# A metaformer layer on one core: the scaling moves to the front of VectorE's step, the square roots to the front of ScalarE's, and the convolution's bands are built inside the first steps

## The chip, the cores and the metric

The kernel runs on one core of a Trainium2 chip. The time is the device time of one execution in microseconds (us), read from the chip; lower is better. Three runs of the kernel before took 4016.77, 4024.47 and 4032.15 us. The engines are called by their short names: PE (TensorE, matmuls), ACT (ScalarE), DVE (VectorE), POOL (GpSimd) and SP (SyncE, which here only issues DMAs). Each runs its own instructions in the order in which they are written and waits for the others on semaphores.

## The reference

Input `x` is 32 images of 112 x 112 pixels with 96 channels, float32.

```
x = x + conv3x3_depthwise(_ln(x)) + _ln(x)     # _ln over the 96 channels, eps 1e-6
t = tokens(x)
h = relu(qlinear(_ln(t, 1e-5), W1, b1))        # 96 -> 384; inputs and weights rounded to 5 exponent, 2 mantissa bits
t = t + qlinear(h, W2, b2)                     # 384 -> 96, the same rounding; sums rounded to 16 bits
```

## The kernel before, in words

An image row index (112) lies on the partitions. A **chunk** is 8 image columns of one image, 112 x 8 x 96 values, 336 KB. An image has 14 chunks, and images go in pairs: 28 chunks (`UNIT`) to a pair, 448 chunks in all.

Each engine runs the same list of **steps** t, and one step works on several chunks at different stages. At step t:
- chunk t+30 is **normalised** for the convolution: DVE takes its mean and variance (`statistics` on `xn`, L582), ACT the square root (`deviation`, L485), DVE the reciprocal (`invert`, L612 to L618), and the eight columns are then written into `images`, columns 0 to 3 by ACT (`normalise`, L465, `ACT_COLS` = 4) and 4 to 7 by DVE (L640). `xn` has two buffers, so a load waits for the chunk before last to be normalised.
- some of the 96 channels of a pair are **convolved** on PE (`conv`, L384), 3 or 4 to a step. For each channel three float32 matmuls (six in the trace) multiply the pair's image by a banded 112 x 112 matrix. The bands of two channels (294 KB) are read from DRAM into a ring of three. ACT saves each finished pair of channels (`save_conv`, L475).
- chunk t-26 gets the convolution added to `x` on POOL (`add_conv`, L224).
- chunk t-28 goes through the **feed-forward**: DVE scales it to 8-bit floats (`scale`, L626), PE transposes it (`to_channels`, L339), ACT copies the result (`copy_xt`, L436), PE multiplies by W1 in three parts (`ffn1`, L352), ACT casts each (`cast_hid`, L444), DVE adds the bias (`add_bias`, L571) and rounds (`quantise`, L577), PE multiplies by W2 in two halves (`ffn2`, L365), ACT casts each (`cast_y`, L452), DVE adds the second bias (`add_y_bias`, L602) and POOL adds the result (`add_ffn`, L230).

Norm steps run from t = -30 to 417, convolutions from -2 to 445, feed-forward from 28 to 475. So there are five **stages**: norm alone (28 steps), norm and convolution (30), all three (t = 28 to 417, 390 steps), convolution and feed-forward (28), feed-forward alone (30).

Within a step the order is that of the code in each engine's `step`. On ACT it is: `copy_xt`, the rest of the last step's saves, `cast_hid` 0, `deviation`, a save, `cast_hid` 1, saves, `cast_y` 0 of the chunk before, `cast_hid` 2, `normalise`, `cast_y` 1. On PE it is: `to_channels`, one channel (of which the last third waits for `copy_xt`, `ffn1_free`), `ffn1` 0 and 1, two channels, `ffn1` 2, `ffn2` 0, any fourth channel, `ffn2` 1. POOL's `add_conv` waits until DVE has added the last bias of the step, and `add_ffn` for `add_y_bias`, so that POOL works beside DVE's `statistics` and `scale`.

Before the steps the banded matrices are built once: PE makes two of their columns for half of the channels at a time (`SETUPS`, L326), DVE and ACT copy them in turn (L563, L429) into the images' second buffer, and SP writes each half (7056 KB) to DRAM (L289). Nothing else may use that buffer meanwhile, and the second half's copies wait for the first half's write.

Of the kernel before, what the change touches and what calls it, by code (L numbers as in the profile page):

```python
# [24 lines left out]
FFN_RING = 7  # L25
ACT_COLS = 4
EPS_C = 1e-6
# [4 lines left out]
def metaformer(nc, x, conv_kernel, w1, b1, w2, b2, bands, out):  # L32
# [13 lines left out]
    with ExitStack() as ctx:  # L46
# [6 lines left out]
        def sem(name):  # L53
# [35 lines left out]
        STAGED_FROM = UNIT  # L89
        band_stage = images[:, 1, :, :, :].rearrange("p i c w -> p (i c w)")[:, 0:NB // 2 * H] \  # L90
            .rearrange("p (g n h) -> p g n h", g=GROUPS // 2, h=H)
        xf_flat = xf[:, :, :, :].rearrange("p r w c -> p (r w c)")
# [28 lines left out]
        band_ps = [bank[0:H, 0:SETUP_COLS * NB // 2] for bank in (conv_ps[:, 0], conv_ps[:, 1], y_ps)]  # L121

# [5 lines left out]
        band_col = [sem("band_col_dve"), sem("band_col_act")]  # L128
        bands_out = [sem(f"bands_out{i}") for i in range(2)]
        xn_in = [sem(f"xn_in{i}") for i in range(NORM_RING)]  # L130
# [54 lines left out]

        with nc.Block() as block:

            @block.gpsimd
            def _(pool):
# [22 lines left out]

                def add_conv(r, c, t):
# [6 lines left out]
                    if ffn_in(t - 1):  # L220
                        wait(pool, hid_biased, J * (LOOP * r + c - FFN_AT))
                    pool.wait_ge(xf_in[e % FFN_RING], dma_count(r, e, FFN_RING))
                    x2 = xf[0:H, e % FFN_RING]
                    pool.tensor_tensor(x2, x2, images[:, b, i, :, cols].rearrange("p c w -> p w c"), ALU.add).then_inc(with_conv, 1)  # L224

                def add_ffn(r, c):
                    e = c - FFN_AT
                    wait(pool, y_biased, LOOP * r + e + 1)
                    res = xf[0:H, e % FFN_RING]
                    pool.tensor_tensor(res, res, y[:, c % 2], ALU.add).then_inc(summed, CW)  # L230
# [10 lines left out]
            def _(sp):  # L241
# [38 lines left out]

                first = NORM_AT - 1
                for half in range(2):
                    for c in range(first, first + 2):
                        step(0, c, c)
                    first += 2
                    for s in band_col:
                        sp.wait_ge(s, SETUPS // 2 * (half + 1))
                    lo = GROUPS // 2 * half
                    sp.dma_start(bands[lo:lo + GROUPS // 2].rearrange("g h n k -> h g n k"), band_stage) \  # L289
                        .then_inc(bands_out[half], 16)  # L290
                for c in range(first, LOOP_AT):
# [14 lines left out]
            def _(pe):  # L306
# [12 lines left out]
                pe.wait_ge(prep, 31)  # L319
                for n in range(2 * SETUPS):  # L320
                    half, i = divmod(n, SETUPS)
                    if n >= 3:
                        pe.wait_ge(band_col[(n - 3) % 2], (n - 3) // 2 + 1)
                    for a in range(SETUP_COLS):
                        h = SETUP_COLS * i + a
                        mm = pe.matmul(band_ps[n % 3][:, NB // 2 * a:NB // 2 * (a + 1)],  # L326
                                       shift[:, H - 1 - h:2 * H - 1 - h],
                                       taps_16[:, NB // 2 * half:NB // 2 * (half + 1)], start=True, stop=True)
                    mm.then_inc(band_mm, 1)
                pe.wait_ge(w_copied, 2)  # L330
                for s in band_col:
                    pe.wait_ge(s, SETUPS)

# [34 lines left out]

                def conv(r, c, ch, next_waits):
                    m = (c - CONV_AT) // UNIT  # L370
                    g, i = divmod(ch, PAIR)
                    n = GROUPS * m + g
                    if i == 0:
                        if g == 0:
                            for s in normed:
                                wait(pe, s, LOOP * r + UNIT * (m + 1))
# [13 lines left out]
                def convs(r, c, t, lo, hi, next_waits=None):  # L390

                    chans = conv_channels(t)[lo:hi]
                    for ch in chans:
                        conv(r, c, ch, next_waits if ch == chans[-1] else None)
# [23 lines left out]
            def _(act):  # L418
# [4 lines left out]
                                     ACT.Identity).then_inc(w_copied, 1)  # L423
                for n in range(1, 2 * SETUPS, 2):
                    i = n % SETUPS
                    act.wait_ge(band_mm, n + 1)
                    if n == SETUPS + 1:
                        act.wait_ge(bands_out[0], 16)
                    nc.scalar.activation(band_stage[:, :, :, SETUP_COLS * i:SETUP_COLS * (i + 1)],  # L429
                                         band_ps[n % 3].rearrange("p (h g n) -> p g n h", h=SETUP_COLS, n=TAPS),  # L430
# [83 lines left out]
            def _(dve):  # L514
# [42 lines left out]
                dve.tensor_copy(b2q[:, :], b2_8).then_inc(prep, 1)  # L557
                for n in range(0, 2 * SETUPS, 2):
                    i = n % SETUPS
                    dve.wait_ge(band_mm, n + 1)  # L560
                    if n == SETUPS:
                        dve.wait_ge(bands_out[0], 16)
                    dve.tensor_copy(band_stage[:, :, :, SETUP_COLS * i:SETUP_COLS * (i + 1)],  # L563
                                    band_ps[n % 3].rearrange("p (h g n) -> p g n h", h=SETUP_COLS, n=TAPS)) \
                        .then_inc(band_col[0], 1)
# [56 lines left out]
                def scale(r, c):  # L622

                    e = c + 1 - FFN_AT
                    for w in range(CW):
                        op = dve.scalar_tensor_tensor(  # L626
                            out=xq_8[:, (c + 1) % 2, w // 2, 0:C, w % 2], in0=xf[0:H, e % FFN_RING, w, :],
                            scalar=stats[:, c % 2, 0, w, 1:2], in1=rstd_t[:, w:w + 1].broadcast_to([H, C]),
                            op0=ALU.subtract, op1=ALU.mult, saturate=False)
# [15 lines left out]
                def step(r, c, t):  # L645
                    now, before, after, norm = ffn_in(t), ffn_in(t - 1), ffn_in(t + 1), norm_in(t)
                    if before:
                        add_bias(r, c - 1, 2)
                    if after or norm:
                        statistics(r, c, t)  # L650
                    if before:
# [12 lines left out]

# [25 lines left out]
```

## Time and profile before

| | |
|---|---|
| median of 3 runs | 4024.47 us |
| the profiled execution | 4024.61 us |
| its span, first to last instruction | 4022.9 us |
| busy: DVE, PE, ACT, POOL | 90%, 78%, 73%, 43% |
| mean granted clock of TensorE | 0.966 of full |
| DMA | 714.60 MB, 178 GB/s over the span |

The busy share of an engine says how long it executed. It doesn't say who waited for whom. For that the profile has a chain of waits: from the last instruction back to what released it, and so on to the start. A timeline row gives the start, how long the group lasted, the engine, the line and, in brackets, how long the engine had been idle and what ended that.

### The profile page before, as it was taken

The numbers are of one execution on the slowest core, as the hardware profiler recorded it, in microseconds if no ns is written. First come the engines' busy times: TensorE is split into PE (matmuls) and PEld (weight loads), VectorE is DVE, ScalarE is ACT, GpSimd is POOL, SyncE is SP. The second block draws the span as 40 slices with busy tenths as digits, with TensorE's granted clock in tenths as the row PEclk, the third lists the DMA queues.
The fourth block names the chain that finished last, engine by engine and source line by source line (L and its number), as shares of the span: only waits on it lengthen the run. The fifth ranks groups of instructions, "written<-read, shape, count | busy, mean of one in ns | idle before, by whom it ended". The sixth has DMA issues, their size and how long they took to land.

```text
span 4022.9 us, 87017 instructions
## 1 busy us (share of the span) xinstructions
PE 3152.2 (78%) x24678; PEld 2482.8 (62%) x24678; DVE 3613.3 (90%) x12635; ACT 2935.4 (73%) x6204; POOL 1720.4 (43%) x915
## 2 busy tenths in 40 slices
PE   3088888878888788888888888888888888889977
PEld 2077666666666666666666666666666666667744
DVE  4647999999999999999999999998999999999998
ACT  3456777777777777777777777777777777777765
POOL 0002444444444444444444444444444444445555
PEclk9999999999999999999999999999999999999955
DMA  4466666666666666666666666666666666665533
GB/s 146 114 170 172 188 188 185 187 184 187 187 185 189 177 190 190 182 180 185 188 185 188 185 186 188 185 188 183 187 189 186 188 185 196 191 191 172 160 106 94
DMA packets 277321, 714.60 MB, mean 178 GB/s; under 512 B 34777, under 2 KB 34882, under 8 KB 276802
## 3 DMA queue, kind: packets, MB, share of 16 engines
q1 hardware_dynamic: 276802, 708.57, 60.1%
q8 instruction: 217, 3.56, 0.4%
q14 instruction: 302, 2.47, 0.2%
HBM read 539.84 MB, written 168.59 MB: 176 GB/s over the span
## 4 chain that ended last, share of the span: by engine, by line
PE 55%; ACT 31%; issue 7%; DMA 5%; DVE 1%; ACTq 1%; SPq 0%; POOLq 0%; POOL 0%; DVEq 0%
PE conv_ps L384 33%; ACT images L465 14%; PE hid_ps L352 13%; ACT hid L444 9%; PE y_ps L365 7%; ACT xt L436 4%; ACT y L452 4%; DMA band_ring<-bands 2%; DMA xn<-in_x 2%; ACTq L167 1%; DMA bands<-images 1%; PE conv_ps L326 1%; DVE stats L582 0%; PE y_ps L326 0%; PE xt_ps L339 0%
## 5 line engine op out<-in xcount | busy, mean ns | idle before, releaser
L384 PE MATMUL conv_ps<-images,band_ring 112*112 112x222 f32 (+1 forms) x9216 | 2064.9, 363 | 604.9 <-ACT xt L436 385.2
L384 PEld LDWEIGHTS conv_ps<-images,band_ring 112*112 112x112 f32 x9216 | 1568.0, 179 | 896.7 <-issue 656.7
L444 ACT ACTIVATE hid<-hid_ps 128x896 f16<-128x896 f32 x1344 | 1226.3, 913 | 505.2 <-PE hid_ps L352 505.2
L224 POOL TENSOR_TENSOR xf<-xf,images 112x768 f32<-112x768 f32 x448 | 980.3, 2188 | 1299.2 <-DVE hid L571 893.7
L230 POOL TENSOR_TENSOR xf<-xf,y 112x768 f32<-112x768 f32 x448 | 736.8, 1645 | 999.3 <-DVE y L602 997.7
L626 DVE SCALAR_TENSOR_TENSOR xq<-xf,stats,xt_ps 112x96 fp8e5<-112x96 f32 x3584 | 844.3, 310 | 0.0
L365 PE MATMUL y_ps<-w2t,hid 128*128 128x96 f16 x10752 | 634.5, 211 | 173.8 <-ACT y L452 172.3
L365 PEld LDWEIGHTS y_ps<-w2t,hid 128*128 128x128 f16 x10752 | 555.1, 100 | 329.0 <-ACT y L452 213.3
L465 ACT ACTIVATE images<-xn,neg_mean,rstd 112x96 f32<-112x96 f32 x1792 | 723.0, 545 | 13.2 <-DVE neg_mean L618 13.2
L352 PE MATMUL hid_ps<-xt,w1t 96*128 96x448 fp8e5 x2688 | 695.6, 369 | 27.7 <-ACT xt L436 19.5
L452 ACT ACTIVATE y<-y_ps 112x384 f16<-112x384 f32 x896 | 443.8, 495 | 364.4 <-PE y_ps L365 362.9
L582 DVE BATCH_NORM_STATS2 stats<-xn 112x6 f32<-112x192 f32 x1792 | 513.5, 348 | 79.5 <-DMA xn<-in_x 77.1
L571 DVE TENSOR_SCALAR hid<-hid,b1q 128x896 f16<-128x896 f16 x1344 | 528.1, 446 | 19.5 <-issue 9.1
L582 DVE BATCH_NORM_STATS2 stats<-xf 112x6 f32<-112x192 f32 x1792 | 510.6, 347 | 0.0
L577 DVE TENSOR_SCALAR hid<-hid 128x2688 uint16<-128x2688 int16 x448 | 505.3, 1128 | 0.1
L640 DVE TENSOR_SCALAR images<-xn,stats,rstd 112x96 f32<-112x96 f32 x1792 | 486.2, 367 | 0.0
L475 ACT ACTIVATE images<-conv_ps 112x448 f32<-112x448 f32 x768 | 414.4, 540 | 79.7 <-PE conv_ps L384 75.4
L352 PEld LDWEIGHTS hid_ps<-xt,w1t 96*128 96x128 f16 x2688 | 263.5, 100 | 237.1 <-ACT hid L444 31.8
L612 DVE RECIPROCAL xt_ps<-std 112x8 f32<-112x8 f32 x448 | 93.5, 209 | 197.2 <-ACT std L485 197.1
L485 ACT ACTIVATE std<-stats,eps 112x8 f32<-112x8 f32 x896 | 225.1, 295 | 57.5 <-DVE stats L582 57.3
L602 DVE TENSOR_TENSOR y<-y,b2q 112x768 f16<-112x768 f16 x448 | 250.7, 559 | 6.7 <-ACT y L452 3.0
L436 ACT ACTIVATE xt<-xt_ps 128x448 uint16<-128x448 uint16 x448 | 235.5, 526 | 11.2 <-PE xt_ps L339 11.2
(46 smaller groups left out, 571.1 us busy)
## 6 DMA issues: line engine op xcount, KB each, us to landing
band_ring<-bands SPq DMA_DIRECT2D x768, 294.0 KB, 5.2
xn<-in_x SPq DMA_DIRECT2D x448, 336.0 KB, 3.5
xf<-in_x SPq DMA_DIRECT2D x448, 336.0 KB, 4.8
out<-xf SPq DMA_DIRECT2D x448, 336.0 KB, 3.9
bands<-images SPq DMA_DIRECT2D x2, 7056.0 KB, 24.5
xf<-in_L_ffn_W SPq DMA_DIRECT2D x2, 144.0 KB, 2.8
xf<-in_L_conv_kernel SPq DMA_DIRECT2D x3, 3.4 KB
xf<-in_L_ffn_b SPq DMA_DIRECT2D x1, 42.0 KB, 3.4
```

The costliest lines, as they stand in the source:

```text
L224: pool.tensor_tensor(x2, x2, images[:, b, i, :, cols].rearrange("p c w -> p w c"), ALU.add).then_inc(with_conv, 1)
L230: pool.tensor_tensor(res, res, y[:, c % 2], ALU.add).then_inc(summed, CW)
L352: mm = pe.matmul(hid_ps[:, k, u, 0:HALF * H], w1t[:, P * j:P * j + P], xt_8[0:C, c % 2, HALF // 2 * u:HALF // 2 * (u + 1)], start=True, st ...
L365: mm = pe.matmul(y_ps[:, C * w:C * w + C], hid[:, c % 2, TOK * j + tok:TOK * j + tok + P], w2t[:, j, :], start=(j == 0), stop=(j == J - 1))
L384: mm = pe.matmul(dst[:, :, lo:hi], band_ring[:, n % BAND_RING, PAIR * dx + i, :], images[:, m % 2, :, ch, lo + dx - 1:hi + dx - 1], start= ...
L444: nc.scalar.activation(hid[:, c % 2, TOK * j:TOK * (j + 1)].rearrange("p (u n) -> p u n", u=2), hid_ps[:, k, :, 0:HALF * H], ACT.Identity) ...
L452: nc.scalar.activation(y[:, c % 2, HALF * u:HALF * u + HALF, :], y_ps[0:H, 0:HALF * C].rearrange("p (w c) -> p w c", c=C), ACT.Identity).t ...
L465: op = nc.scalar.activation(images[:, b, i, :, cols.start + w], xn[:, e % NORM_RING, w, :], ACT.Identity, bias=neg_mean[:, c % 2, w:w + 1] ...
L571: dve.tensor_scalar(part_j, part_j, b1q[:, j:j + 1], None, ALU.add).then_inc(hid_biased, 1)
L577: dve.tensor_scalar(bits.bitcast(U16), bits.bitcast(I16), ROUND8, -ROUND8, ALU.add, ALU.add).then_inc(hid_quant, 1)
L582: op = dve.bn_stats(stats[:, c % 2, i, w:w + 2, :].rearrange("p w s -> p (w s)"), src[:, w:w + 2, :].rearrange("p w c -> p c w"))
L626: op = dve.scalar_tensor_tensor(out=xq_8[:, (c + 1) % 2, w // 2, 0:C, w % 2], in0=xf[0:H, e % FFN_RING, w, :], scalar=stats[:, c % 2, 0, w ...
```

## The change

1. DVE's step. `scale` of a chunk ran at the end of the step before the one in which PE transposes it. It now runs in the same step, right behind `statistics`; it uses the statistics and reciprocals of the step before. The three `add_bias` of the chunk before come behind it together, then `quantise`, `invert`, `add_y_bias` and `normalise`.
2. ACT's step. `deviation` goes from behind `cast_hid` 0 to the front, ahead of `copy_xt`.
3. `ACT_COLS` goes from 4 to 5: ACT normalises five columns, DVE three.
4. POOL's step. `add_ffn` comes first and is one step later (chunk t-31); it waits until DVE has normalised the chunk before. `add_conv` follows and no longer waits for the bias.
5. The bands are built inside the first 23 norm steps, five setups to a step, four columns for a quarter of the channels each. The staging area holds two quarters, and SP writes four quarters (3528 KB each) to DRAM.

```diff
-ACT_COLS = 4
+ACT_COLS = 5
...
-        SETUP_COLS = 2
+        SETUP_COLS = 4
         SETUPS = H // SETUP_COLS
+        STEP_SETUPS = 5
...
+        def setups(c, t):
+            n = STEP_SETUPS * (t - NORM_AT)
+            return range(n, min(n + STEP_SETUPS, QUARTERS * SETUPS)) if c == t and n >= 0 else range(0)
...
-                def add_ffn(r, c):
-                    e = c - FFN_AT
+                def add_ffn(r, c, t):
+
+                    e = c - 3 - FFN_AT
+                    if norm_in(t - 1):
+                        wait(pool, normed[1], LOOP * r + c - NORM_AT)
                     wait(pool, y_biased, LOOP * r + e + 1)
...
                 def step(r, c, t):
+                    if ffn_in(t - 3):
+                        add_ffn(r, c, t)
                     if ffn_in(t + 2):
-                        add_conv(r, c, t)
-                    if ffn_in(t - 2):
-                        add_ffn(r, c - 2)
+                        add_conv(r, c)
...
+                    if c in done:
+                        q = done[c]
+                        for s in band_col:
+                            sp.wait_ge(s, SETUPS // 2 * (q + 1))
+                        sp.dma_start(bands[QGROUPS * q:QGROUPS * (q + 1)].rearrange("g h n k -> h g n k"),
+                                     band_stage[:, q % 2]).then_inc(bands_out[q], 16)
...
                     now, before, norm = ffn_in(t), ffn_in(t - 1), norm_in(t)
+                    for n in setups(c, t):
+                        if n % 2:
+                            build(n)
+                    if ffn_in(t + 1) or norm:
+                        deviation(r, c, t)
                     if now:
                         copy_xt(r, c)
                     save_conv(r, c - 1, t - 1, 3, C)
                     if now:
                         cast_hid(r, c, 0)
-                    if ffn_in(t + 1) or norm:
-                        deviation(r, c, t)
...
-                    if before:
-                        add_bias(r, c - 1, 2)
                     if after or norm:
                         statistics(r, c, t)
+                    for n in setups(c, t):
+                        if n % 2 == 0:
+                            build(n)
+                    if now:
+                        scale(r, c)
                     if before:
+                        for j in range(J):
+                            add_bias(r, c - 1, j)
                         quantise(r, c - 1)
                     if after or norm:
                         invert(r, c, t)
                     if ffn_in(t - 2):
                         add_y_bias(r, c - 2)
-                    if after:
-                        scale(r, c)
                     if norm:
                         normalise(r, c)
-                    if now:
-                        add_bias(r, c, 0)
-                        add_bias(r, c, 1)
```

On ACT, one step of the stage with all three, before (the rows L167 are register operations and waits of the sequencer; `std` is `deviation`, `xt` is `copy_xt`, `hid` is `cast_hid`, `images<-xn` is `normalise`):

```order
L452 ACTIVATE y<-y_ps 112x384 [waits y_mm]
L436 ACTIVATE xt<-xt_ps 128x448 [waits xt_mm]
L167 ISA
L167 ISA [waits hid_mm]
L444 ACTIVATE hid<-hid_ps 128x896 [waits y_mm]
L167 REGISTER_ALU
L485 ACTIVATE std<-stats,eps 112x8 [waits stats_done]
L485 ACTIVATE std<-stats,eps 112x8
```

The same place on ACT after the change:

```order
L461 ACTIVATE y<-y_ps 112x384 [waits y_mm]
L171 REGISTER_ALU
L494 ACTIVATE std<-stats,eps 112x8 [waits stats_done]
L494 ACTIVATE std<-stats,eps 112x8
L445 ACTIVATE xt<-xt_ps 128x448 [waits xt_mm]
L171 ISA
L171 ISA [waits hid_mm]
L453 ACTIVATE hid<-hid_ps 128x896 [waits y_mm]
```

The two square roots now stand between the last `cast_y` of one step and the `copy_xt` of the next.

On DVE, the same stage after the change, from the statistics to the normalising (before, `xq`, which is `scale`, stood between the `y` addition and `images<-xn`, and two of the three `hid<-hid,b1q` behind that):

```order
L594 BN_STATS stats<-xf 112x6 x3
L638 SCALAR_TENSOR_TENSOR xq<-xf,stats,xt_ps 112x96 x8
L171 ISA
L583 TENSOR_SCALAR hid<-hid,b1q 128x896 [waits hid_cast]
L171 REGISTER_ALU
L583 TENSOR_SCALAR hid<-hid,b1q 128x896 [waits hid_cast]
L171 REGISTER_ALU
L583 TENSOR_SCALAR hid<-hid,b1q 128x896 [waits hid_cast]
L589 TENSOR_SCALAR hid<-hid 128x2688 [waits hid_biased]
L171 REGISTER_ALU [waits xt_copied]
L624 RECIPROCAL xt_ps<-std 112x8 [waits std_done]
```

The reciprocals' wait for `xt_copied` now asks for the copy of a chunk that was scaled in the same step.

## Rows read from the trace of the kernel before

**Rows 1.** Page, part 1: busy time and share of the span of each engine.

```profile
PE 3152.2 (78%) x24678; PEld 2482.8 (62%) x24678; DVE 3613.3 (90%) x12635; ACT 2935.4 (73%) x6204; POOL 1720.4 (43%) x915
```

**Rows 2.** Page, part 4: the chain of waits, by engine and by line.

```profile
PE 55%; ACT 31%; issue 7%; DMA 5%; DVE 1%; ACTq 1%; SPq 0%; POOLq 0%; POOL 0%; DVEq 0%
PE conv_ps L384 33%; ACT images L465 14%; PE hid_ps L352 13%; ACT hid L444 9%; PE y_ps L365 7%; ACT xt L436 4%; ACT y L452 4%; DMA band_ring<-bands 2%; DMA xn<-in_x 2%; ACTq L167 1%; DMA bands<-images 1%; PE conv_ps L326 1%; DVE stats L582 0%; PE y_ps L326 0%; PE xt_ps L339 0%
```

**Rows 3.** Busy us by stretch: length, PE, PEld, DVE, ACT, POOL; clock, DMA, GB/s.

```profile
353.00:3603.00 3250.00, 2628.76 (x21158) 2091.34 (x21157) 3033.44 (x10854) 2498.66 (x5317) 1481.82 (x774) 0.99 0.64 186
```

**Rows 4.** The chain in order of time, one step: start, us, what.

```profile
2019.83 0.62 PE conv_ps L384 x2
2020.45 0.76 PE hid_ps L352 x4
2021.21 2.26 PE conv_ps L384 x12
2023.47 0.38 PE hid_ps L352 x2
2023.85 0.53 PE y_ps L365 x12
...
2027.60 0.43 ACT xt L436
...
2028.15 0.62 PE conv_ps L384 x2
```

**Rows 5.** Timeline of the same step, with rows of ACT, DVE and POOL.

```profile
2020.82 0.95 DVE L577 TENSOR_SCALAR hid<-hid 128x2688 uint16<-128x2688 int16 x1
...
2022.29 0.21 DVE L612 RECIPROCAL xt_ps<-std 112x8 f32<-112x8 f32 x1 [0.52 <-ACT std L485]
...
2024.98 1.08 DVE L640 TENSOR_SCALAR images<-xn,stats,rstd 112x96 f32<-112x96 f32 x4
...
2025.66 1.61 ACT L465 ACTIVATE images<-xn,neg_mean,rstd 112x96 f32<-112x96 f32 x4
...
2027.10 0.50 ACT L452 ACTIVATE y<-y_ps 112x384 f16<-112x384 f32 x1
2027.19 2.18 POOL L224 TENSOR_TENSOR xf<-xf,images 112x768 f32<-112x768 f32 x1 [2.14 <-DVE hid L571]
...
2030.09 0.49 ACT L485 ACTIVATE std<-stats,eps 112x8 f32<-112x8 f32 x2
2030.48 0.53 ACT L475 ACTIVATE images<-conv_ps 112x448 f32<-112x448 f32 x1
```

**Rows 6.** Timeline of the start: bands, first norm steps, first convolution.

```profile
13.31 0.72 PE L326 MATMUL conv_ps<-xf 67*112 67x144 bf16 x4 [5.34 <-DVE xf L546]
...
75.61 1.14 DVE L582 BATCH_NORM_STATS2 stats<-xn 112x6 f32<-112x192 f32 x4
...
109.07 1.15 DVE L582 BATCH_NORM_STATS2 stats<-xn 112x6 f32<-112x192 f32 x4 [19.93 <-DMA xn<-in_x]
...
178.42 1.15 DVE L582 BATCH_NORM_STATS2 stats<-xn 112x6 f32<-112x192 f32 x4 [1.07 <-DMA xn<-in_x]
...
185.31 1.15 DVE L582 BATCH_NORM_STATS2 stats<-xn 112x6 f32<-112x192 f32 x4 [1.01 <-DMA xn<-in_x]
...
193.93 9.01 PE L384 MATMUL conv_ps<-images,band_ring 112*112 112x224 f32 x36 [118.44 <-DMA band_ring<-bands]
```

**Rows 7.** Page, part 6: DMA issues, KB each, us from issue to landing.

```profile
xn<-in_x SPq DMA_DIRECT2D x448, 336.0 KB, 3.5
...
bands<-images SPq DMA_DIRECT2D x2, 7056.0 KB, 24.5
```

**Rows 8.** Timeline, feed-forward alone: `quantise` begun while POOL adds.

```profile
3902.72 2.00 DVE L577 TENSOR_SCALAR hid<-hid 128x2688 uint16<-128x2688 int16 x1
```

**Rows 9.** PE's timeline in the second stage, behind a wait for bands.

```profile
299.04 13.19 PE L384 MATMUL conv_ps<-images,band_ring 112*112 112x224 f32 x60 [2.50 <-DMA band_ring<-bands]
```

**Rows 10.** Busy time by stretch, just behind that wait.

```profile
300.00:304.00 4.00, 4.00 (x15) 3.38 (x14) 2.05 (x8) 1.50 (x4) 0.00 (x0) 0.57 0.59 167
```

More of the change, by code:

```diff
@@ L89, in metaformer @@
         STAGED_FROM = UNIT
-        band_stage = images[:, 1, :, :, :].rearrange("p i c w -> p (i c w)")[:, 0:NB // 2 * H] \
-            .rearrange("p (g n h) -> p g n h", g=GROUPS // 2, h=H)
+        QUARTERS = 4
+        QGROUPS = GROUPS // QUARTERS
+        QB = NB // QUARTERS
+        band_stage = images[:, 1, :, :, :].rearrange("p i c w -> p (i c w)")[:, 0:2 * QB * H] \
+            .rearrange("p (s g n h) -> p s g n h", s=2, g=QGROUPS, h=H)
         xf_flat = xf[:, :, :, :].rearrange("p r w c -> p (r w c)")
@@ L118, in metaformer @@
         b2_8 = staged(H, C).bitcast(F8)[:, 0:C]
-        SETUP_COLS = 2
+        SETUP_COLS = 4
         SETUPS = H // SETUP_COLS
-        band_ps = [bank[0:H, 0:SETUP_COLS * NB // 2] for bank in (conv_ps[:, 0], conv_ps[:, 1], y_ps)]
+        STEP_SETUPS = 5
+        band_ps = [bank[0:H, 0:SETUP_COLS * QB] for bank in (conv_ps[:, 0], conv_ps[:, 1], y_ps)]
         w1_in, w2_in, small_in, taps_sem = sem("w1_in"), sem("w2_in"), sem("small_in"), sem("taps_in")
@@ L128, in metaformer @@
         band_col = [sem("band_col_dve"), sem("band_col_act")]
-        bands_out = [sem(f"bands_out{i}") for i in range(2)]
+        bands_out = [sem(f"bands_out{i}") for i in range(QUARTERS)]
         xn_in = [sem(f"xn_in{i}") for i in range(NORM_RING)]
@@ L278, in step @@
                                 .then_inc(band_in[n % BAND_RING], 16)
[L281 to L291, printed above, removed]
+                done = {(SETUPS * (q + 1) - 1) // STEP_SETUPS + NORM_AT: q for q in range(QUARTERS)}
+                for c in range(NORM_AT - 1, LOOP_AT):
                     if c == CONV_AT - 1:
@@ L319, in _, with build @@
                 pe.wait_ge(prep, 31)
-                for n in range(2 * SETUPS):
-                    half, i = divmod(n, SETUPS)
+                pe.wait_ge(w_copied, 2)
+                def build(n):
+                    q, i = divmod(n, SETUPS)
                     if n >= 3:
@@ L325, in _ @@
                         h = SETUP_COLS * i + a
-                        mm = pe.matmul(band_ps[n % 3][:, NB // 2 * a:NB // 2 * (a + 1)],
-                                       shift[:, H - 1 - h:2 * H - 1 - h],
-                                       taps_16[:, NB // 2 * half:NB // 2 * (half + 1)], start=True, stop=True)
+                        mm = pe.matmul(band_ps[n % 3][:, QB * a:QB * (a + 1)], shift[:, H - 1 - h:2 * H - 1 - h],
+                                       taps_16[:, QB * q:QB * (q + 1)], start=True, stop=True)
                     mm.then_inc(band_mm, 1)
-                pe.wait_ge(w_copied, 2)
-                for s in band_col:
-                    pe.wait_ge(s, SETUPS)
                 def to_channels(r, c):
@@ L367, in ffn2, with conv @@
                     mm.then_inc(y_mm, 1)
-                def conv(r, c, ch, next_waits):
+                def conv(r, c, t, ch, next_waits):
                     m = (c - CONV_AT) // UNIT
@@ L374, in conv @@
                         if g == 0:
+                            if t == CONV_AT:
+                                for s in band_col:
+                                    pe.wait_ge(s, QUARTERS * SETUPS // 2)
                             for s in normed:
@@ L393, in convs @@
                     for ch in chans:
-                        conv(r, c, ch, next_waits if ch == chans[-1] else None)
+                        conv(r, c, t, ch, next_waits if ch == chans[-1] else None)
                     if next_waits and not len(chans):
@@ L423, in _, with build @@
                                      ACT.Identity).then_inc(w_copied, 1)
-                for n in range(1, 2 * SETUPS, 2):
-                    i = n % SETUPS
+                def build(n):
+                    q, i = divmod(n, SETUPS)
                     act.wait_ge(band_mm, n + 1)
-                    if n == SETUPS + 1:
-                        act.wait_ge(bands_out[0], 16)
-                    nc.scalar.activation(band_stage[:, :, :, SETUP_COLS * i:SETUP_COLS * (i + 1)],
+                    if q >= 2 and i == 1:
+                        act.wait_ge(bands_out[q - 2], 16)
+                    nc.scalar.activation(band_stage[:, q % 2, :, :, SETUP_COLS * i:SETUP_COLS * (i + 1)],
                                          band_ps[n % 3].rearrange("p (h g n) -> p g n h", h=SETUP_COLS, n=TAPS),
@@ L557, in _, with build @@
                 dve.tensor_copy(b2q[:, :], b2_8).then_inc(prep, 1)
-                for n in range(0, 2 * SETUPS, 2):
-                    i = n % SETUPS
+                def build(n):
+                    q, i = divmod(n, SETUPS)
                     dve.wait_ge(band_mm, n + 1)
-                    if n == SETUPS:
-                        dve.wait_ge(bands_out[0], 16)
-                    dve.tensor_copy(band_stage[:, :, :, SETUP_COLS * i:SETUP_COLS * (i + 1)],
+                    if q >= 2 and i == 0:
+                        dve.wait_ge(bands_out[q - 2], 16)
+                    dve.tensor_copy(band_stage[:, q % 2, :, :, SETUP_COLS * i:SETUP_COLS * (i + 1)],
                                     band_ps[n % 3].rearrange("p (h g n) -> p g n h", h=SETUP_COLS, n=TAPS)) \
@@ L622, in scale @@
                 def scale(r, c):
-                    e = c + 1 - FFN_AT
+                    e = c - FFN_AT
                     for w in range(CW):
                         op = dve.scalar_tensor_tensor(
-                            out=xq_8[:, (c + 1) % 2, w // 2, 0:C, w % 2], in0=xf[0:H, e % FFN_RING, w, :],
-                            scalar=stats[:, c % 2, 0, w, 1:2], in1=rstd_t[:, w:w + 1].broadcast_to([H, C]),
+                            out=xq_8[:, c % 2, w // 2, 0:C, w % 2], in0=xf[0:H, e % FFN_RING, w, :],
+                            scalar=stats[:, (c - 1) % 2, 0, w, 1:2], in1=rstd_t[:, w:w + 1].broadcast_to([H, C]),
                             op0=ALU.subtract, op1=ALU.mult, saturate=False)
@@ L646, in step @@
                     now, before, after, norm = ffn_in(t), ffn_in(t - 1), ffn_in(t + 1), norm_in(t)
-                    if before:
-                        add_bias(r, c - 1, 2)
                     if after or norm:
                         statistics(r, c, t)
+                    for n in setups(c, t):
+                        if n % 2 == 0:
+                            build(n)
+                    if now:
+                        scale(r, c)
                     if before:
+                        for j in range(J):
+                            add_bias(r, c - 1, j)
                         quantise(r, c - 1)
```

9 lines of the change are left out of this document (4 added, 5 removed).

## Prediction

> **What bounds the kernel now.** I read the busy shares first, then the chain of waits, then one step of the chain against the timeline. The busy shares say DVE: 90% of the span [rows 1], and in the stage where all three kinds of work run, 3033 of 3250 us [rows 3]. The chain of waits says something else: PE 55%, ACT 31%, DVE 1% [rows 2]. DVE is busy, and almost nothing that ends last goes through it.
>
> The Trainium skill (Perfetto Trace Analysis, Identifying the Most-Contended Engine) has you take the engine with the highest occupancy and optimise that one first. That would be DVE. This trace doesn't bear it out, and that is the main choice of this prediction.
>
> One step of the chain shows why. `copy_xt` ends on ACT and PE, held at the last third of its first channel, goes on at 2019.83: 0.62 us of convolution, 0.76 of `ffn1` 0 and 1, 2.26 of two channels, 0.38 of `ffn1` 2, 0.53 of `ffn2` 0 [rows 4], together 4.55 us with no gap. Then ACT takes over and works through, in its own order, `cast_y` 0, `cast_hid` 2, the four columns of `normalise`, `cast_y` 1 and the next `copy_xt`, whose link begins at 2027.60, and PE goes on at 2028.15. That is a closed loop of 2028.15 - 2019.83 = 8.32 us, and there is nothing in it that waits for DVE. 390 steps of 8.32 are 3245 us, which is the length of the stage [rows 3]: the loop is the stage. DVE itself waits in each step, 0.52 us for the square roots [rows 5]; its own work is 8.32 - 0.52 = 7.80 us.
>
> Two things of ACT's are outside the loop today. The saves stand in places where ACT waits for PE, and so does `deviation`: it sits behind `cast_hid` 0, where ACT has time until `ffn2` 0 is done. Moving it costs or brings something only by where it lands.
>
> **The change part by part.** *`deviation` to the front of ACT's step.* It now stands between `cast_y` 1 and `copy_xt`, both links of the loop. From the start of the two square roots to the start of what follows them it is 2030.48 - 2030.09 = 0.39 us [rows 5]. Its input is there: DVE's statistics end some 2 us into its step and ACT comes to it later. ACT has no wait in that part of the loop that could swallow it, so +0.39 us a step. The bounds: 0 if ACT waited at that place for PE's transposes, 0.49 (the row's whole duration) if nothing overlaps. I take 0.39.
>
> *A fifth column on ACT.* Four columns take 2027.10 - 2025.66 = 1.44 us from start to start [rows 5], 0.36 each, all of it in the loop: +0.36 us. Bounds 0.36 and 1.61 / 4 = 0.40. DVE loses one of four columns, 1.08 / 4 = 0.27 us [rows 5], off the loop: nothing.
>
> *`scale` behind the statistics, biases together.* On DVE this only reorders; its work becomes 7.80 - 0.27 = 7.53 us, and its wait for the square roots goes. What it must deliver in time is `scale` before `to_channels` and `quantise` before `ffn2` 0. `scale` ends about 4 us into DVE's step and the transposes follow at once, while ACT reaches `copy_xt` only after the square roots; `quantise` ends about 2 us after `scale`, and PE comes to `ffn2` 0 4.0 us of its own work behind `copy_xt`. Neither is late. `invert` now waits for the `copy_xt` of the same step; what is queued behind it on DVE is the second bias, three columns and the next statistics, and ACT needs the reciprocals only for `normalise`, some 6 us later. So: nothing gained, since the loop doesn't use DVE, and nothing lost while DVE's 7.53 us plus new stalls stay under the loop's length.
>
> *POOL.* Its two additions, 1.64 and 2.18 us, now run one behind the other from the end of DVE's normalising. They are beside statistics and `scale`, together about 4 us. Where they run over, DVE's bias or rounding is held: `quantise` takes 2.00 us [rows 8] when it begins beside POOL's addition and 0.95 otherwise [rows 5]. A late `xf` would do it. One such stall a step, 1.05 us, makes DVE 8.6 us, still under the new loop. Nothing; it is at the edge of mattering.
>
> *The `xn` load.* A chunk's load is issued once ACT has normalised the chunk two before it, and lands 3.5 us later [rows 7]. From there DVE needs statistics, `scale` and the transposes, about 4.5 us, before `copy_xt`: 8 us, against one loop and the `cast_y` and square roots before it, about 9.8 us. Hidden, by less than 2 us. SP's queue: the output's DMA now waits for an addition made in the same step, and the `xf` and band loads stand behind it; but SP waits longer at the `xn` load ahead of all three, so that wait hides the other.
>
> So a step of the main stage becomes 8.32 + 0.39 + 0.36 = 9.07 us. Times 390: 0.75 x 390 = +292 us.
>
> *The other stages.* In the two without normalising only one square root is moved, half of 0.39, in 58 steps: at most 11 us where ACT's turn is in the chain; I take +8 (bounds 0 and 11). In the second stage the chain passes ACT's columns only now and then: between 0 and 30 x 0.36 = 11 us, I take +5.
>
> *The bands.* Before: from 13.31 to 75.61 they are built, 62.3 us, of which 24.5 is the wait for the first half's write [rows 7]; from 75.61 to 193.93 the 28 norm steps, 118.3 us, with 19.93 of waiting behind the second write [rows 6]. Two norm steps take 185.31 - 178.42 = 6.89 us [rows 6]. After: if the building hides wholly in the norm steps' waits, 28 x (3.45 + 0.18) = 102 us, plus four writes of a quarter, each 12.2 us by size, of which 24.5 - 19.93 = 4.6 are covered as today: 4 x 7.7 = 31. With the first load that is some 135 us in place of 180.6, a gain of 46. If it adds to them wholly, 62.3 - 24.5 = 37.8 us come back, a gain of 8. The setups now hold four small matmuls in place of two, which no row prices; DVE's and ACT's copies alternate and so wait for each other. I take the middle, -25 (bounds -46 and -8, and 0 if the small matmuls bound it).
>
> **The sum**, against the profiled execution, 4024.61 us (0.1 us above the median; the span is 1.7 less): 4024.6 + 292 + 8 + 5 - 25 = 4305 us, 7% slower.
>
> **The rivals.** *DVE bounds it.* This is what the skill's rule on occupancy would give; worked out from rows: with the wait gone and a column less the step is 7.53 us, 0.79 less, 390 x 0.79 = 308 us, and with the bands 4024.6 - 308 - 25 = 3692 us. For it: 90% busy, and 0.52 us of waiting in each step. Against it: the chain, and that DVE's wait is for ACT, which the change makes later and not earlier in the loop. 6%.
>
> *Half of the cost is hidden.* If PE's transposes come late, ACT would have waited at `copy_xt` and the square roots fill that time: only the column counts, 0.36 x 390 = 140, and 4024.6 + 140 + 13 - 25 = 4153 us. Against it: before, ACT doesn't wait there. 6%.
>
> *The two halves cancel.* If the square roots are hidden and the column's end is where PE waits anyway, the sum is the bands' alone, near 4005 us. 2%.
>
> *PE's clock falls.* The main stage has a granted clock of 0.99 [rows 3]. In the second stage, behind a wait of 2.50 us, a stretch had 0.57 [rows 9, 10], a mix of the full and the half level. PE's wait for `copy_xt` grows by up to 0.75 us in each step. If the clock came to 0.9 on average, PE's 4.55 us would be 0.5 longer: 390 x 0.5 = +197, near 4500 us. Against it: today's gaps in the main stage, over a microsecond each, left it at 0.99. It decides from the point where the gap gets as long as the one in that row. 5%.
>
> **How the numbers follow.** The forecast has 81%: 4305 us. Its own range is 4240 to 4385: a step cost of 0.65 to 0.90 (254 to 351 us; the ends are small overlaps, and a stall of DVE that shows) and the bands. With a part of the clock's case and of the hidden half the range is 4200 to 4400, which leaves out under 2 in 10. A difference of 0.5%, 20 us, is about what a measurement of this kernel can tell from none. Slower by more: 81 + 6 + 5 = 92%. Faster by more: 6%. Between: 2%.
>
> **What would show it.** Right: in the main stage `copy_xt` follows its neighbour every 9.0 to 9.1 us; the chain still has PE and ACT, now with the square roots' line at 4% and the columns' line near 17%; DVE's busy share falls to about 83% although its work is hardly changed, with waits for `xt_copied` or `xn`; the first convolution starts near 170 us. Wrong: a step below 8.3 us with DVE without waits (then DVE was the bound); the square roots missing from the chain; ACT waiting for the transposes (PE's line L339 before `copy_xt`); a granted clock well under 0.99 in that stage; the first convolution after 194 us.

## The result

| | us |
|---|---|
| before, median of 4 runs | 4020.62 |
| changed, median of 4 runs (4662.08 to 4752.31) | 4694.22 |
| ratio | 1.165, 95% interval 1.159 to 1.171 |
| forecast (range) | 4305 (4200 to 4400) |
| profiled execution of the changed kernel, and its span | 4708.99, 4707.3 |

The change makes the kernel 16.5% slower. The sign was forecast, the size was not: 674 us were lost, 280 were foreseen, and the time lies outside the range. One of the four runs of the changed kernel, 4752.31 us, lies more than 1.5% above the fastest and is left out of the ratio; the median of the other three is 4679.44, and the differences to other runs below are taken from it.

The page of the changed kernel, busy shares and the chain of waits, beside [rows 1, 2]:

```profile
PE 3576.7 (76%) x24902; PEld 2754.8 (59%) x24902; DVE 3721.2 (79%) x12187; ACT 3100.4 (66%) x6652; POOL 1725.4 (37%) x915
...
PEclk9998888888888989899888999889898888989965
...
PE 52%; ACT 32%; issue 8%; DMA 3%; DVE 3%; ACTq 1%; POOL 1%; SPq 0%; POOLq 0%; DVEq 0%
PE conv_ps L391 33%; PE hid_ps L356 13%; ACT images L474 13%; ACT hid L453 7%; PE y_ps L369 6%; ACT xt L445 4%; ACT y L461 4%; ACT std L494 3%; DMA xn<-in_x 2%; DMA band_ring<-bands 1%; DVE stats L594 1%; ACTq L171 1%; POOL xf L229 1%; DVE xq L638 1%; DVE images L652 0%
```

The square roots (L494) are in the chain now, as forecast. The surprise is the clock row: it is 8 or 9 tenths through the main stage, which before had 0.99 [rows 3]. The stretch that answers to it (length, busy us of PE, PEld, DVE, ACT, POOL, then clock, DMA share, GB/s):

```profile
353.00:4280.00 3927.00, 3029.13 (x21070) 2334.12 (x21069) 3153.48 (x10423) 2639.80 (x5681) 1486.64 (x773) 0.89 0.52 153
```

One step of the chain in order of time (start, us, what), beside [rows 4]:

```profile
2023.00 0.62 PE conv_ps L391 x2
2023.63 0.76 PE hid_ps L356 x4
2024.38 2.26 PE conv_ps L391 x12
2026.64 0.38 PE hid_ps L356 x2
2027.02 0.53 PE y_ps L369 x12
...
2030.81 0.32 ACT y L461
2031.13 0.39 ACT std L494 x2
2031.51 0.43 ACT xt L445
2031.95 0.12 issue
2032.07 0.62 PE conv_ps L391 x2
```

PE's links are those of before to the hundredth. ACT's have the two square roots between `cast_y` 1 and `copy_xt`, and 2032.07 - 2023.00 = 9.07 us, which is the forecast step. But not every step is like this. Of 388 intervals between successive `copy_xt` in the main stage, 174 are 8.9 to 9.1 us, 160 are 10.4 to 10.8 and 46 are 12.2 to 12.4; the mean is 10.17 (before: 8.37, of which 375 of 388 are 8.2 to 8.4). This is how a longer one begins, in PE's rows of the timeline; after the shape stands the idle time before, and what ended it. The first three rows are of a step two earlier and come into play below:

```profile
2020.40 0.37 PE L343 MATMUL xt_ps<-ident,xq 112*128 112x112 bf16 x4 [0.59 <-DVE xq L638]
...
2023.00 0.62 PE L391 MATMUL conv_ps<-images,band_ring 112*112 112x222 f32 x2 [1.43 <-ACT xt L445]
...
2024.22 2.42 PE L391 MATMUL conv_ps<-images,band_ring 112*112 112x224 f32 x12
...
2038.55 0.37 PE L343 MATMUL xt_ps<-ident,xq 112*128 112x112 bf16 x4 [0.60 <-DVE xq L638]
2038.76 0.97 PE L391 MATMUL conv_ps<-images,band_ring 112*112 112x224 f32 x4
2041.14 1.08 PE L391 MATMUL conv_ps<-images,band_ring 112*112 112x222 f32 x2 [1.41 <-ACT xt L445]
2042.01 1.70 PE L356 MATMUL hid_ps<-xt,w1t 96*128 96x448 fp8e5 x4
2043.50 4.45 PE L391 MATMUL conv_ps<-images,band_ring 112*112 112x224 f32 x12
2047.79 0.54 PE L356 MATMUL hid_ps<-xt,w1t 96*128 96x448 fp8e5 x2
```

and the granted clock (the third number from the end) in stretches of both:

```profile
2022.00:2024.00 2.00, 1.00 (x5) 0.66 (x6) 1.74 (x6) 0.87 (x4) 0.00 (x0) 1.00 0.50 81
2024.00:2026.00 2.00, 2.00 (x13) 1.85 (x11) 1.34 (x6) 1.88 (x3) 1.05 (x1) 1.00 1.00 393
...
2038.00:2040.00 2.00, 1.18 (x8) 0.80 (x8) 1.97 (x7) 2.00 (x7) 0.82 (x1) 1.00 0.00 0
2040.00:2042.00 2.00, 0.86 (x2) 0.60 (x3) 1.52 (x5) 1.01 (x4) 0.00 (x0) 0.70 0.44 58
2042.00:2044.00 2.00, 2.00 (x7) 1.20 (x6) 1.36 (x6) 0.92 (x2) 0.92 (x1) 0.50 1.01 379
```

The twelve convolution matmuls take 4.45 us in place of 2.42 because the clock fell to its lower level (0.50 is 1.2 of 2.4 GHz). They are links of the loop, so the whole delay goes into the step. Before it fell PE had been idle twice, 0.60 us for `scale` and 1.41 for `copy_xt`; but two steps earlier it had been idle for 0.59 and 1.43 us at the same places, and the clock stayed at 1.00. Three steps earlier one longer wait had done nothing either; the clock's stretches from 2012 to 2020 show 1.00:

```profile
2013.93 0.62 PE L391 MATMUL conv_ps<-images,band_ring 112*112 112x222 f32 x2 [1.84 <-ACT xt L445]
```

The trace settles whether the longer steps are those with a fallen clock. All of the 214 have the lower level in them, for 1.6 us or more; of the 174 others eight have, for 0.5 us each. The 214 are together 429 us longer than 9.07 us each. The kernel before had 13 steps over 9.5 us, 12 of them with a fall: 27 us together with the stage's first.

In sum, by the starts of `copy_xt`: the first comes at 331.2 us in place of 351.0 (-20), the 390th at 4285.1 in place of 3611.6 (3954 against 3261 us, +693), and from there to the end of the span it is 422 against 411 us (+11). Together +684, the difference of the two spans. Of the 693 us, 0.75 x 390 = 292 are the forecast step and some 400 (429 - 27) the steps with a fallen clock.

### The profile page after: what moved, and what is told of

It is laid out like the page before. It is cut to its first block, busy times and chain, and to the rows that moved or that the text cites. A ratio compares the mean times of both kernels' runs of the same rounds, so it can differ in the third digit from the quotient of the medians.

```text
span 4707.3 us, 87416 instructions
## 1 busy us (share of the span) xinstructions
PE 3576.7 (76%) x24902; PEld 2754.8 (59%) x24902; DVE 3721.2 (79%) x12187; ACT 3100.4 (66%) x6652; POOL 1725.4 (37%) x915
## 4 chain that ended last, share of the span: by engine, by line
PE 52%; ACT 32%; issue 8%; DMA 3%; DVE 3%; ACTq 1%; POOL 1%; SPq 0%; POOLq 0%; DVEq 0%
PE conv_ps L391 33%; PE hid_ps L356 13%; ACT images L474 13%; ACT hid L453 7%; PE y_ps L369 6%; ACT xt L445 4%; ACT y L461 4%; ACT std L494 3%; DMA xn<-in_x 2%; DMA band_ring<-bands 1%; DVE stats L594 1%; ACTq L171 1%; POOL xf L229 1%; DVE xq L638 1%; DVE images L652 0%
## 5 line engine op out<-in xcount | busy, mean ns | idle before, releaser
L391 PE MATMUL conv_ps<-images,band_ring 112*112 112x222 f32 (+1 forms) x9216 | 2362.7, 401 | 701.8 <-ACT xt L445 621.0
L391 PEld LDWEIGHTS conv_ps<-images,band_ring 112*112 112x112 f32 x9216 | 1790.8, 204 | 1071.8 <-issue 770.6
L453 ACT ACTIVATE hid<-hid_ps 128x896 f16<-128x896 f32 x1344 | 1200.8, 914 | 605.4 <-PE hid_ps L356 605.4
L474 ACT ACTIVATE images<-xn,neg_mean,rstd 112x96 f32<-112x96 f32 x2240 | 883.6, 544 | 14.2 <-DVE neg_mean L630 14.2
L583 DVE TENSOR_SCALAR hid<-hid,b1q 128x896 f16<-128x896 f16 x1344 | 782.4, 624 | 113.3 <-ACT hid L453 110.1
L356 PE MATMUL hid_ps<-xt,w1t 96*128 96x448 fp8e5 x2688 | 818.3, 422 | 33.1 <-ACT xt L445 24.8
L356 PEld LDWEIGHTS hid_ps<-xt,w1t 96*128 96x128 f16 x2688 | 293.8, 111 | 302.8 <-issue 109.7
L652 DVE TENSOR_SCALAR images<-xn,stats,rstd 112x96 f32<-112x96 f32 x1344 | 381.1, 368 | 29.5 <-POOL xf L229 29.4
L589 DVE TENSOR_SCALAR hid<-hid 128x2688 uint16<-128x2688 int16 x448 | 390.9, 873 | 15.3
L343 PE MATMUL xt_ps<-ident,xq 112*128 112x112 bf16 x1792 | 172.3, 221 | 131.3 <-DVE xq L638 127.0
L494 ACT ACTIVATE std<-stats,eps 112x8 f32<-112x8 f32 x896 | 223.4, 293 | 29.1 <-DVE stats L594 22.9
```

Source lines behind the costliest of these rows:

```text
L356: mm = pe.matmul(hid_ps[:, k, u, 0:HALF * H], w1t[:, P * j:P * j + P], xt_8[0:C, c % 2, HALF // 2 * u:HALF // 2 * (u + 1)], start=True, st ...
L391: mm = pe.matmul(dst[:, :, lo:hi], band_ring[:, n % BAND_RING, PAIR * dx + i, :], images[:, m % 2, :, ch, lo + dx - 1:hi + dx - 1], start= ...
L453: nc.scalar.activation(hid[:, c % 2, TOK * j:TOK * (j + 1)].rearrange("p (u n) -> p u n", u=2), hid_ps[:, k, :, 0:HALF * H], ACT.Identity) ...
L474: op = nc.scalar.activation(images[:, b, i, :, cols.start + w], xn[:, e % NORM_RING, w, :], ACT.Identity, bias=neg_mean[:, c % 2, w:w + 1] ...
L583: dve.tensor_scalar(part_j, part_j, b1q[:, j:j + 1], None, ALU.add).then_inc(hid_biased, 1)
```

## The experiments

Theory 1 is the prediction's loop of ACT and PE with the clock added to it: what the change puts into the loop costs 0.75 us a step, and PE's longer idle times let the clock fall, which costs the rest. The rivals are that DVE bounds the kernel, and that the slow steps come from a late load or from DVE's and POOL's new order. Ratios are to the kernel before on the same chip, with 95% intervals.

**A column less on ACT.**

```diff
-ACT_COLS = 5
+ACT_COLS = 4
```

> The changed kernel with ACT_COLS back at 4. Theory 1 (a closed loop of ACT and PE sets the step, 0.39 us of square roots and 0.36 us of a fifth column are in it, and PE's longer idle time lets its clock fall in some steps): the undisturbed step is 9.07 - 0.36 = 8.71 us, PE waits 0.3 to 0.4 us less for copy_xt, the granted clock lies between 0.89 and 0.97, time 4200 to 4450 us. Theory 2 (DVE, POOL or a late load sets the slow steps): DVE has a column more, 0.27 us, and the time stays within 1% of 4690 us or grows.

Measured: 4251.16 us, ratio 1.056 (1.051 to 1.061), clock 0.945 over the span. 307 of the steps are 8.6 to 8.7 us, the mean is 9.02. As theory 1 has it: one column is worth 428 us, of which 140 by the step's length and the rest by the clock (65 steps are over 9.5 us here, 64 of them with a fall, and 214 in the changed kernel).

**More work for PE while it waits.**

```diff
                     for dx in (1, 0, 2):
                         if dx == 2 and next_waits:
+                            if busy:
+                                keep_busy(n % 2)
                             next_waits()
...
+                def keep_busy(k):
+                    for _ in range(24):
+                        pe.matmul(conv_ps[:, k, PAIR * IMGS * W:], ident[:, :], ident[:, 0:512 - PAIR * IMGS * W],
+                                  start=True, stop=True, skip_group_check=True)
```

(`busy` is true for the first channel of a step in the main stage. The extra matmuls write spare columns of the bank in which the channel is being summed. With them the kernel's output is wrong, by a relative error of 0.34; why was not followed up, and this run and the two like it are read for time alone.)

> The changed kernel, with 24 extra matmuls (128 x 128 by 64 columns, results unused) on PE in every step of the main stage, placed just before PE waits for copy_xt. They add work and no dependence. Theory 1: PE's idle time there falls from 1.4-1.8 us to a few tenths, the granted clock is 0.97 or more, nearly every step is 9.07 us, time 4280 to 4330 us. Theory 2 (the slow steps come from a late load or from DVE and POOL, and the clock falls because PE then waits): the steps of 10.4 to 12.3 us stay, time within 1% of 4690 us or more.

Measured: 4325.95 us, 1.074 (1.070 to 1.079), clock 0.964. 351 of 388 steps are 8.9 to 9.1 us. PE's rows of one step in its timeline:

```profile
2014.43 0.37 PE L343 MATMUL xt_ps<-ident,xq 112*128 112x112 bf16 x4 [0.41 <-DVE xq L645]
2014.64 0.97 PE L398 MATMUL conv_ps<-images,band_ring 112*112 112x224 f32 x4
2015.45 0.86 PE L355 MATMUL conv_ps<-ident 128*128 128x64 bf16 x24
2016.86 0.62 PE L398 MATMUL conv_ps<-images,band_ring 112*112 112x222 f32 x2 [0.55 <-ACT xt L452]
2017.32 0.92 PE L361 MATMUL hid_ps<-xt,w1t 96*128 96x448 fp8e5 x4
2018.08 2.42 PE L398 MATMUL conv_ps<-images,band_ring 112*112 112x224 f32 x12
```

PE does 0.86 us more work in every step and the kernel is 353 us faster. Nothing in the loads, DVE's order or POOL's was touched. This is the run that tells the clock from the other causes: with PE kept busy nearly all the slow steps are gone.

**The control: the same extra matmuls in the kernel before.** The edit is the one above.

> The kernel before with the same 24 extra matmuls in each step of the main stage: the control for the run that added them to the changed kernel. Theory 1 (they act through the clock alone): before has few steps with a fallen clock, so at most those go; the step stays 8.32 us, time between 0 and 25 us below before. If the extra matmuls brought time in some other way, or cost it, this run would show it: over 0.6% faster, or slower.

Measured: 4049.02 us, 1.007 (1.005 to 1.009), clock 0.966. It was slower, which I had not expected: the extra matmuls cost 30 us here, some steps being 8.5 to 9.2 us. They bring nothing by themselves. Without that cost, if it is the same there, the changed kernel with its clock kept up would be near 4326 - 30 = 4296 us; the forecast without the clock's case was 4305.

**Five columns in the kernel before, no order changed.**

```diff
-ACT_COLS = 4
+ACT_COLS = 5
```

> The kernel before with ACT_COLS = 5 and nothing else: no engine's order is changed, and DVE has less work. Theory 1: the undisturbed step is 8.32 + 0.36 = 8.68 us, at least 390 x 0.36 = 140 us slower; PE's wait for copy_xt grows by as much and some steps lose more by the clock, time 4160 to 4400 us. Theory 2 (DVE bounds the kernel before, and the slow steps come from the new order): 0.27 us less on DVE, time 3920 to 4030 us, clock as before.

Measured: 4300.3 us, 1.069 (1.065 to 1.073), clock 0.938. 240 steps are 8.7 us, 73 are 10.4, and every step over 9.5 us has a fall of the clock in it. DVE had less to do and the kernel was 280 us slower: DVE doesn't bound it, and the clock falls without any of the new orders.

**The same with the extra matmuls.**

> The kernel before with ACT_COLS = 5 and the 24 extra matmuls in each step of the main stage. Theory 1: without the extra matmuls this kernel was at 4300 us, of which 390 x 0.36 = 140 us is the column and some 140 us the clock. With them the undisturbed step is 8.68 to 8.75 us, steps of 10 us and more become few, time 4165 to 4210 us. Rival (the 10 us steps have another cause): 4300 us or, with the cost of the extra matmuls, 4330 us.

Measured: 4184.74 us, 1.041 (1.039 to 1.043), clock 0.967; 304 steps of 8.7 us. 116 us come back. Less the 30 of the control it is 4155, against 4018 + 140 for the column alone. So in this kernel too the column's cost is half its own length and half the clock.

**`deviation` back at its old place in the changed kernel.**

```diff
                 def step(r, c, t):
...
-                    if ffn_in(t + 1) or norm:
-                        deviation(r, c, t)
                     if now:
                         copy_xt(r, c)
                     save_conv(r, c - 1, t - 1, 3, C)
                     if now:
                         cast_hid(r, c, 0)
+                    if ffn_in(t + 1) or norm:
+                        deviation(r, c, t)
```

> The changed kernel with deviation back behind cast_hid 0, all else as changed. If the 0.39 us of the square roots were all that its new place costs, the step is 9.07 - 0.39 = 8.68 us and the time near that of the kernel before with five columns, 4300 us. But with DVE's new order a second loop closes: scale 1.88, transposes 0.41, copy 0.64, PE to the end of ffn1 0 1.2, cast_hid 0.81, square roots 0.54, reciprocals to normalise 1.6, statistics 2.1, and scale again, 9.2 us. Theory 1 expects that loop to end last: an undisturbed step of 9.1 to 9.3 us, DVE waiting for the square roots and no longer for xt_copied, the clock as low as in the changed kernel or lower, time 4650 to 4850 us.

Measured: 4681.24 us, 1.166 (1.162 to 1.169), clock 0.869. 105 steps are 9.2 us and 87 are 9.3 to 9.4. The waits (who waited for what: us in total between 500 and 3500, times, longest):

```profile
DVE xt_ps L624 <- ACT std L494: 696.7, 298, 3.2
PEld xt_ps L343 <- DVE xq L638: 523.6, 293, 2.7
PE xt_ps L343 <- DVE xq L638: 514.5, 298, 7.7
```

The second loop is there, with the length worked out from rows: `scale`, transposes, copy, `ffn1`, cast, square roots, reciprocals, statistics, `scale`. So the 0.39 us can't simply be undone. With DVE's new order the square roots are either ahead of `copy_xt`, in ACT's loop, or behind it, in DVE's. The prediction hadn't seen this.

**The bands alone.** The bands are built inside the steps as in the change; `ACT_COLS` and every engine's order are those of before.

> The bands built inside the first 23 norm steps, in quarters, with all engines' step orders and ACT_COLS = 4 as before: the one part of the change that brought time. Theory 1: the first convolution starts near 170 us in place of 194, later stages are unchanged, time 15 to 30 us below the kernel before (3990 to 4005 us). Rival: the gain of 20 us at the start is given back in the second stage, where PE waits for bands, and the time is within 5 us of before.

Measured: 3994.0 us, 0.993 (0.991 to 0.996). The first convolution starts at 164.5 us (changed kernel: 168.4, before 193.9 [rows 6]). This part of the change is a gain of 0.7% by itself.

**One column less than before on ACT, one more on DVE**, on the kernel with the bands in the steps (`ACT_COLS = 3`).

> The kernel before with the bands built in the steps, and three columns on ACT, five on DVE. Theory 1: the loop loses 0.36 us (7.96 us), DVE gains 0.27 (7.80 to 8.07 us) and so ends last; step 8.05 to 8.15 us, DVE's wait for the square roots nearly 0, time 3890 to 3920 us. Rival (DVE bounds the kernel before): 390 x 0.27 = 105 us slower than the 3994 us of the same kernel with four columns.

Measured: 3862.17 us, 0.962 (0.960 to 0.965); 312 steps of 8.0 us. It is 28 us below the forecast's low end. The chain, by engine:

```profile
DVE 69%; PE 15%; issue 7%; ACT 4%; DMA 3%; SPq 0%; DVEq 0%; ACTq 0%; POOLq 0%
```

More work on the engine that was 90% busy made the kernel 3.3% faster, until most of the chain went through that engine. The median step is 7.97 us, where DVE had been expected at 8.07 and the loop of ACT and PE at 7.96. Two things explain the tenth: a column costs DVE 0.24 us from start to start and not the 0.27 of the row, and DVE's own work is nearer 7.74 than 7.80, as the next run shows. The two loops are level here.

**Two of ACT's four columns where ACT waits**, on the kernel with the bands in the steps (`normalise` now takes the bounds of its columns).

```diff
+                    if norm:
+                        normalise(r, c, 0, 2)
                     if before:
                         cast_y(r, c - 1, 0)
                     if now:
                         cast_hid(r, c, 2)
                     if norm:
-                        normalise(r, c)
+                        normalise(r, c, 2, ACT_COLS)
```

> The kernel before with the bands built in the steps, and two of ACT's four normalising columns moved ahead of cast_y 0, into the time in which ACT waits for ffn2 0 (nothing is added or taken away). Theory 1 (ACT's columns are in the loop only because of where they stand): two columns, 0.72 us, leave the loop, which would be 7.6 us; DVE's own work of 7.80 us then ends last, so the step is 7.8 to 7.9 us, DVE's wait for the square roots goes to nearly 0, PE waits less and the clock stays, time 3790 to 3830 us. Rival (any work of ACT is on the path, wherever it stands): the step stays 8.32 us, time 3994 us.

Measured: **3784.07 us, 0.942 (0.939 to 0.945)**, the fastest kernel of the study. ACT's and DVE's rows at that place in its timeline:

```profile
2011.70 0.20 DVE L627 RECIPROCAL xt_ps<-std 112x8 f32<-112x8 f32 x1
...
2012.49 0.90 ACT L474 ACTIVATE images<-xn,neg_mean,rstd 112x96 f32<-112x96 f32 x2
...
2013.54 0.49 ACT L460 ACTIVATE y<-y_ps 112x384 f16<-112x384 f32 x1 [0.15 <-PE y_ps L368]
2013.93 0.91 ACT L452 ACTIVATE hid<-hid_ps 128x896 f16<-128x896 f32 x1
```

The two columns stand where ACT had waited for `ffn2` 0 (in the kernel before 267.4 us in 357 waits between 500 and 3500, 0.75 us each); 0.15 of that wait is left. DVE hardly waits for the square roots any more, 16 us in all between 500 and 3300 us. The mean step is 7.84 us, the median 7.74, and DVE, with 57% of the chain, now ends last in most places; 7.80 for its own work was a little too much. Nothing was taken away: the same instructions on the same engines, two of them a place earlier.

**Three of five columns there.** As above with `ACT_COLS = 5` and `normalise(r, c, 0, 3)` first.

> As the run with two columns moved ahead of cast_y 0, but ACT_COLS = 5 and three of the five moved. Theory 1: the ACT and PE loop is 8.32 + 0.36 - 3 x 0.36 = 7.6 us, DVE's own work 7.80 - 0.24 = 7.56 us; the two are now equal, so a step of 7.6 to 7.85 us and 3700 to 3790 us, at most a few per cent below the 3784 us of the run with two columns. Rival (ACT's own work, 6.4 + 0.4 us and its waits, ends last once more than two columns stand there): slower than that run, 3790 to 3900 us.

Measured: 3837.21 us, 0.955 (0.953 to 0.957). It is slower than the run before it, as the rival had it, and the chain goes through ACT (44%) and hardly through DVE (6%). 157 of 388 steps are 7.6 us, as the two loops allow, and 136 are 8.2. In the one step of the chain that I followed, a save stands ahead of the three columns and ACT has no wait left to hide the third in; that this is the cause in all 136 was not tried.

## Why the prediction was wrong

*What bounds the kernel: right.* DVE, 90% busy, was off the path. It is shown from both sides: less work for DVE and more for ACT cost 7%, more for DVE and less for ACT brought 3.3%. The rival by the Trainium skill's rule on occupancy (Perfetto Trace Analysis, Identifying the Most-Contended Engine), 3692 us, failed with it.

*The step of 9.07 us: right.* It is the length of the undisturbed step to the hundredth, by 0.39 for the square roots and 0.36 for the column, 8.72 with the column left out of the change, and 8.68 with the column alone in the kernel before. The square roots alone were not run: their 0.39 is read from the chain and is what remains above 8.32 in the changed kernel with four columns (0.40). One sign was off all the same: the columns' line has 13% of the chain, as against the near 17% that was named.

*PE's clock: here it failed.* The sum has no term for it: the case was left among the rivals with 5% and a price of 197 us, and it cost some 400. Two things were wrong in it. The weight: "Against it: today's gaps in the main stage, over a microsecond each, left it at 0.99. It decides from the point where the gap gets as long as the one in that row", the one of 2.50 us [rows 9, 10]. The length of a single wait was the wrong thing to compare: the fall shown above came behind waits of 0.60 and 1.41 us, while waits of 0.59 and 1.43 two steps earlier, and one of 1.84 three steps earlier, had no fall behind them. And the 0.99 didn't say that those gaps left the clock up: it had fallen in a few steps of the kernel before too. In the changed kernel PE also waits for `scale` before the transposes, which the text had called not late, in 135 of the some 295 steps between 500 and 3500 us, 0.7 us each on average; but the clock fell as well in the kernel before with five columns, whose order of `scale` is the old one. What the kernels with many falls have in common is that PE's same work is spread over a longer round. Why one round keeps its clock and the next does not these runs don't settle. And the price: I took a mean clock of 0.9, which is what came (0.89), but charged it on 4.55 us of PE's links as if it were spread evenly over the step. In the step shown it lies on the links, where the twelve matmuls take 4.45 us in place of 2.42, and 214 of 388 steps paid 1.3 to 3.3 us each: 429 us for some 880 us at the lower level, nearly the half that they would pay if PE's links filled all of it. That is some 400 us more than before and not 197.

*DVE's order: nothing gained, nothing lost in the step, as forecast, but with two things unseen.* DVE's work was put at 7.53 us a step and measures 3153 / 390 = 8.1. Its `add_bias` takes 0.62 us on average and took 0.45 before: in the main stage 351 of 1158 are mostly beside one of POOL's additions, at 0.98 us each, and the 783 clear of them take 0.44. That was below the loop's length and cost nothing. Nor is the new order neutral. By putting `scale` behind the statistics it opens PE's wait for the transposes, and it closes a second loop of 9.2 us for which `deviation` had to go to the front.

*POOL and the `xn` load.* DVE waited for `xn`, 0.7 us in many steps, and POOL for `xf`, and neither set an undisturbed step. Right.

*The bands: right in the sum, by luck in the parts.* First convolution forecast near 170 us, measured 168.4; -20 us to the first `copy_xt` against -20 in the sum (-25 for the bands, +5 behind them). With the bands alone the first `copy_xt` comes at 320.0 us, so they bring 31 and what stands behind them costs 11; both terms were 6 us short and cancel. The last stages were put at +8 and came to +11.

## What to carry to other kernels

When the chain of waits is a closed loop of two engines, price a change by what it puts between the links, and not by busy shares; work placed where an engine waits is free as far as that wait reaches (two columns were, a third was not), and the same work a few places later costs its whole length. Then look at the clock: here, when the loop got longer by work on another engine, PE was idle for longer in every round, its clock fell more often, and then its own links got longer too. For a kernel whose matmuls are in the loop I would now take that case as a main one whenever PE's idle share rises, even if each single wait stays short.

## What the runs showed of the hardware that I had not expected

- The granted clock of the main stage fell from 0.99 to 0.89 when the undisturbed step grew from 8.32 to 9.07 us with the same work on PE; with the step at 8.7 us the span's mean was 0.938 and 0.945, against 0.966. The length of the waits just before doesn't tell: a fall came behind 0.60 and 1.41 us, and none behind 0.59 and 1.43 two steps earlier nor behind a single 1.84.
- 24 extra matmuls of 0.86 us in all, in each step, made a kernel 353 us faster (4679 to 4326) and another 116 us (4300 to 4185), and cost the kernel whose clock had been up 30 us.
- A normalising instruction of DVE takes 0.37 us as a row but 0.24 from start to start; four in a row show 1.08 us.
- DVE's `add_bias` (128 x 896, 16-bit) took 0.44 us clear of POOL's additions and 0.98 when mostly beside one (changed kernel, main stage).
